# Fused attention on one NeuronCore: where a unit's second score stands, and the order of maxima, exponentials and emptyings

## The reference, cut to what matters

```python
qkv = x @ W_qkv                       # 16 heads of 64
attn = jnp.einsum('bqhd,bkhd->bhqk', q, k) * DH ** -0.5
attn = jax.nn.softmax(attn, axis=-1)  # over 1024 keys
out  = jnp.einsum('bhqk,bkhd->bqhd', attn, v).reshape(Bq, Tq, INNER)
```

## Time and profile before

| what | value |
|---|---|
| median of 3 runs | 2981.74 us (2980.43 to 2981.94) |
| span of the profiled execution, first to last instruction | 2977.2 us |
| median less span | 4.5 us |
| attention stage in the trace | about 943 to 2094 us |
| TensorE busy in the span | 2911.4 us, 98% |
| VectorE | 2235.5 us, 75% |
| ScalarE | 1608.2 us, 54% |

### The profile page before, as it was taken

How to read it: one execution, slowest core, us unless ns; L and a number is a source line. 1 busy time by engine, 2 the same in 40 slices (tenths; PEclk the granted TensorE clock), 3 DMA queues, 4 the chain that set the end, 5 groups by cost and what they waited for, 6 DMA issues and landing times. The chain is left out here.

```text
span 2977.2 us, 68699 instructions
## 1 busy us (share of the span) xinstructions
PE 2911.4 (98%) x27938; PEld 2491.7 (84%) x27938; DVE 2235.5 (75%) x3109; ACT 1608.2 (54%) x3315; POOL 989.3 (33%) x641
## 2 busy tenths in 40 slices
PE   8999999999998999999999999999999999979998
PEld 5999889999987777777777777777788999979998
DVE  4589886655535888888888888888577766588876
ACT  2366654333212777777777777777233555554443
POOL 1011110000001444444444444446465555533332
PEclk9999999999999999999999999999999999999999
DMA  5643327563596333333333333332663555587775
GB/s 183 224 161 108 118 78 254 216 216 117 180 309 183 112 94 98 93 87 87 87 87 94 87 94 87 93 96 78 206 229 141 199 192 202 199 276 213 244 247 173
DMA packets 283011, 464.50 MB, mean 156 GB/s; under 512 B 34968, under 2 KB 156984, under 8 KB 278360
## 3 DMA queue, kind: packets, MB, share of 16 engines
q1 hardware_dynamic: 273844, 453.88, 47.1%
q0 software_dynamic: 576, 6.29, 0.6%
q10 hardware_dynamic: 8292, 0.05, 0.2%
HBM read 277.21 MB, written 182.92 MB: 155 GB/s over the span
## 5 line engine op out<-in xcount | busy, mean ns | idle before, releaser
L1817 DVE TENSOR_REDUCE b_nm<-b_ps 128x1 f32<-128x1024 f32 x512 | 601.7, 1217 | 17.5 <-PE b_ps L1758 4.1
L1726 ACT ACTIVATE b_p<-b_ps,b_nm 128x1024 f32<-128x1024 f32 x512 | 564.9, 1113 | 8.5 <-DVE b_nm L1817 8.5
L1787 PE MATMUL b_po<-b_pt,b_v 128*64 128x256 f32 x4096 | 498.3, 385 | 0.8 <-DVE b_pt L1837 0.8
L1731 ACT ACTIVATE b_pt<-b_tp_act 128x512 f32<-128x512 f32 x512 | 308.2, 602 | 305.0 <-PE b_tp_dve L1770 305.0
L1837 DVE COPY b_pt<-b_tp_dve 128x512 f32<-128x512 f32 x512 | 351.1, 686 | 117.4 <-PE b_tp_dve L1770 117.3
L1770 PEld LDWEIGHTS b_tp_act<-ident,b_p 64*128 64x128 f32 x4096 | 311.7, 138 | 124.1 <-issue 100.7
L1787 PEld LDWEIGHTS b_po<-b_pt,b_v 128*64 128x64 f32 x4096 | 271.9, 136 | 128.7 <-ACT b_pt L1731 0.9
L1770 PE MATMUL b_tp_act<-ident,b_p 64*128 64x64 f32 x4096 | 347.6, 225 | 2.4 <-issue 2.4
L1770 PE MATMUL b_tp_dve<-ident,b_p 64*128 64x64 f32 x4096 | 348.0, 225 | 0.0
L1770 PEld LDWEIGHTS b_tp_dve<-ident,b_p 64*128 64x128 f32 x4096 | 312.0, 138 | 8.6
L2297 POOL TENSOR_TENSOR d_blocks<-d_blocks 128x512 f32<-128x512 f32 x128 | 183.0, 1430 | 162.3 <-ACT d_blocks L2343 155.4
(11 more groups left out here) (418 smaller groups left out, 7710.2 us busy)
## 6 DMA issues: line engine op xcount, KB each, us to landing
b_raw_q<-q_t SPq DMA_DIRECT2D x124, 256.0 KB, 4.2
x_mlp_raw<-hidden_blocks SPq DMA_DIRECT2D x112, 256.0 KB, 3.6
d_x_second_raw<-hidden_blocks SPq DMA_DIRECT2D x112, 256.0 KB, 3.1
hidden_blocks<-d_blocks SPq DMA_DIRECT2D x32, 768.0 KB, 3.5
k_t<-p_out SPq DMA_DIRECT2D x64, 256.0 KB, 2.2
q_t<-p_out SPq DMA_DIRECT2D x64, 256.0 KB, 2.3
v_n<-p_out SPq DMA_DIRECT2D x64, 256.0 KB, 3.7
b_v<-v_n SPq DMA_DIRECT2D x32, 512.0 KB, 3.9
```

What stands on the lines that cost most here:

```text
L1726: act.activation(pr[k % 4][:], ps[k % 2][:], ACT.Exp, bias=nm[:, k % 4:k % 4 + 1], accum_out=rs[:, n:n + 1]).then_inc(exp_done, 1)
L1731: act.activation(dst, src, ACT.Copy).then_inc(t_out[0], 1)
L1787: mm = pe.matmul(po[rows, (blk % 2) * 2 * P:(blk % 2 + 1) * 2 * P], vt[u][:, kc, rows], pt[blk % 2][h][:, kc, :], start=(kc == 0), stop=(k ...
L1817: dve.tensor_reduce(nm[:, k % 4:k % 4 + 1], ps[k % 2][:], axis=AX.X, op=ALU.max, negate=True).then_inc(max_done, 1)
```

## The change

It reorders three queues and adds or removes no instruction:

```diff
 ScalarE pair_step(i, k):
     empty(i, k)
-    for j in (k, k + 1):
-        if more(i, j + 2):
-            exp(i * TS + j + 2, j + 2)
+    if more(i, k + 2):
+        exp(i * TS + k + 2, k + 2)
     empty(i, k + 1)
+    if more(i, k + 3):
+        exp(i * TS + k + 3, k + 3)

 TensorE pair_step(i, k):
-    for j in (k, k + 1):
-        if more(i, j + 2):
-            scores(i, j + 2)
+    if more(i, k + 2):
+        scores(i, k + 2)
     transposes(i, k)
     block_values(i, k)
+    if more(i, k + 3):
+        scores(i, k + 3)
     transposes(i, k + 1)

 VectorE pair_step(i, k):
-    for j in (k, k + 1):
-        if more(i, j + 2):
-            maximum(i * TS + j + 2, j + 2)
+    if more(i, k + 2):
+        maximum(i * TS + k + 2, k + 2)
     empty(i, k)
     if k % QB == 2 and k >= QB:
         output(i, k // QB - 1)
+    if more(i, k + 3):
+        maximum(i * TS + k + 3, k + 3)
     empty(i, k + 1)
     if k % STEPS == STEPS - 2:
         inverses(i, k // STEPS)
```

## The result

The changed kernel takes 3056.28 us (median of 4, 3055.96 to 3060.45) against 2981.09 us: 75.2 us slower, ratio 1.0256 with a 95% interval of 1.0243 to 1.0269. The forecast was 3052 us, its range 3003 to 3080.

What follows compares the result with a forecast made beforehand. Attention was taken as bound by a chain of TensorE alone, 4.46 us per unit; a, b and c add 0.55 us per block, x 128 = 70 us, giving 3052 us with span-to-median 4.5; range 3003 to 3080.

Steps and rivals of the forecast that it cites:

- The unit is a chain of TensorE alone: In attention, only what lengthens TensorE's own steps or makes it wait counts; a unit is 4.46 us, 256 units 1142 us.
- a: TensorE's steps get new neighbours, a score behind V instead of transposes: +0.03 us per unit, +8 us in all.
- rivals 1 and 2: Score's weights load ahead behind V: waits bind, 3005 us, chance 0.08 (first); waits don't reach TensorE, 2943, chance 0.05 (second).
- b: Transposes T(k) wait for ScalarE's emptying of the single bank `tp_act`: 0.21 us in every unit.
- Rival 3: The waits stay hidden and only the changed neighbours cost: +8 us, 2990 us, chance 0.03.
- c: V half 0 waits for VectorE's emptying in every second unit: 0.05 to 0.08 us per block beside b, 0.29 alone.
- The sum: Per block of two units b 0.42, c 0.05 to 0.08, a 0.07: 0.55 us, x 128 blocks = 70 us.
- The slacks: ScalarE is free 1.1 us before T(k+1) ends; the exponential signals 0.7 us before the score reusing its buffer starts.
- rival 4: More is lost: TensorE waits for an exponential's rest, or idle times lower the clock; about 3095 us, chance 0.05.

Runs made afterwards that it cites:

- the control: The kernel before with both engines' emptyings cut to 2 of 8 column groups from the ninth step on: 2980.98 us, ratio 0.9996.
- The last experiment: The changed kernel with VectorE's emptying k+1 put ahead of maximum k+3: 3055.41 us, ratio 1.0242.

## Why the prediction was right, step by step

- *The unit is a chain of TensorE alone.* Right: the control with copies cut to a quarter stays at 2981.
- *a, neighbours, +8 us.* 7.6 in medians (4.8 to 11.6), 12 by the units inside attention: 0.05 a unit instead of 0.03. V to score came to 0.30 or 0.31 like V to transpose. The score behind it took 0.57, not 0.56. The early weight load of the Trainium skill ("TensorE: Matmul & The Clock Gate", Part 2, "Step-by-step") did not reach across V to a score, even with no wait left (both copies short), so rivals 1 and 2 fell together. Why it did not is not shown.
- *b, 0.21 in every unit, 54 us.* Measured 52.5 with c absent. The chain 0.22 + 0.05 + 0.60 + 0.10 = 0.97 is met to the hundredth, though its last term came from a single wait at attention's start. Rival 3, waits hidden, fell with it.
- *c, 0.05 to 0.08 in every second unit.* This is the term that was mis-sized. It is 0.25 - 0.15 = 0.10 in the trace, and by the runs 13.5 us (3056.28 - 3042.74; 15.1 when each is set against the kernel before as measured beside it), 0.105 per block. The 0.03 that I took off for a quicker V wasn't there: V took the same 1.57 from first to last matmul behind either wait. Alone c is worth 39.1 us where 0.29 x 128 = 37 was worked out.
- *The sum*, 0.55 per block, was 0.60; most of the difference is c. In spans that is 77.0 us where 70 was forecast. The medians differ by 75.2 only: 4.5 us stood between the span and the median of three runs before (3.9 with the fourth), 2.1 after, and the forecast had carried the 4.5 over unchanged. That 3052 is within 4.3 us of the result is in part luck.
- *The slacks.* Right for the changed kernel: 5 waits for an exponential, all near the start. The last experiment shows how thin they are: 1.1 us of delay of one maximum used them up.
- *Clock.* 1.00 as before; rival 4 fell. The Trainium skill's second way of losing the clock ("TensorE: Matmul & The Clock Gate", Part 1, "A second HAM failure mode"), by short idle times between groups of matmuls, did not occur at stops of 0.16 us. Between 1000 and 2000 us only the kernel with ScalarE's order put back was below 1.00.
- *What the profile would show.* The distances were right, but I said that TensorE would be seen idle behind ScalarE's copy. It isn't: the stop hides under the recorded length of the score's matmul and appears as "issue" on the load row. The prediction also named as a sign of its failure that TensorE's idle time in attention stays as it was. By the matmul rows it nearly does: 1151 - 1145.2 = 5.8 us before, 1226 - 1218.1 = 7.9 after. The stage is 75 us longer all the same, so the sign was badly chosen, and the distances are what bears the theory out.

## What to carry to other kernels

When an order written out by hand is changed around an engine that never waits, write down, for each single buffer, the distance between its two users before and after, and set it against the chain "last write, handover, copy, handover". Two such chains that met in one place overlapped here (91.6 us apart, 67.6 together), so test them together as well as apart; and an emptying that is moved behind work of a later step must be followed to every buffer it frees, the doubled ones too. A busy share that stays at 98% does not say that an engine isn't waiting: compare distances from start to start.

## What the runs showed of the hardware that I had not expected

Stops are given here as start-to-start distance less the 0.23 of the last score matmul. With stops of 2.0 us in a unit of 6.58 us the granted clock of the stage averaged 0.96, in stretches of 200 us 0.96 to 0.97 each (one run). With stops of 1.04 us in a unit of 5.67 (VectorE's order put back) it stayed at 1.00, and so it did with stops of 1.7 and 1.2 us in turn in units of 6.23 and 5.76 (TensorE's order put back, one run).

A copy of a quarter of the columns takes somewhat under half the time: ScalarE 593 ns for 512 columns and 272 for 128, VectorE 681 and 281.

The change of neighbour has a price of its own. A score or a transpose behind V starts 0.30 to 0.31 behind V's last matmul, where V's own matmuls stand 0.22 apart, and it then takes 0.06 to 0.10 longer than elsewhere (transposes 0.49 instead of 0.43, a score 0.57 instead of 0.47 behind another score).
